# First attention of a two-layer network: projections spaced by three slots, masks and row normalisation moved to GpSimd

## The reference, cut to what matters

```
x = x + _L0_attn_ref(_layernorm(x), w_qkv, b_qkv, w_out, b_out)

def _L0_attn_ref(x, w_qkv, b_qkv, w_out, b_out):          # 16 heads of 16
    q, k, v = jnp.split(x @ w_qkv + b_qkv, 3, axis=-1)
    dot = jnp.einsum('bhid,bhjd->bhij', q, k)
    vals = q_norm_sq + k_norm_sq.transpose(0, 1, 3, 2)
    scores = dot * dot / (vals - 2.0 * dot + EPSILON)
    scores = scores + mask                                # -1e9 above the diagonal
    attn = jax.nn.softmax(scores, axis=-1)
    out = jnp.einsum('bhij,bhjd->bhid', attn, v)
    return out @ w_out + b_out
```

## Time and profile before

| What | Value |
|---|---|
| median of 3 runs | 2801.84 us (2799.59 to 2802.47) |
| the profiled execution, whole | 2797.78 us |
| its span in the trace | 2796.0 us |
| mean granted TensorE clock | 0.976 of full speed |
| busy shares over the span: PE, DVE, ACT, POOL | 94%, 82%, 74%, 65% |
| first `weigh` and last `weigh` of the first attention | 44.12 us and 1295.09 us |

### The profile page before, as it was taken

One profiled execution on the slowest core, in us unless ns is written; L12 is line 12 of the kernel. 1 busy time (PEld: TensorE's weight loads), 2 busy tenths in 40 slices (PEclk: granted clock), 3 DMA queues, 4 the chain that ended last, 5 costly groups with the idle time before them and its releaser, 6 DMA issues. The chain is left out here.

```text
span 2796.0 us, 75274 instructions
## 1 busy us (share of the span) xinstructions
PE 2615.3 (94%) x27044; PEld 1818.8 (65%) x27044; DVE 2280.6 (82%) x6931; ACT 2078.2 (74%) x3782; POOL 1811.9 (65%) x3152
## 2 busy tenths in 40 slices
PE   5999999999999999997889789999999999699999
PEld 3677777777777777775333257777777777466766
DVE  5999999999999999986655468888888888488998
ACT  4998899999998999895333257667677776478886
POOL 3767666777667766774421157677777767588885
PEclk8999999999999999999899889999999999899999
DMA  4334433444334433441000166655556664000001
GB/s 116 68 62 77 79 61 62 74 80 79 61 64 80 73 61 62 72 72 47 10 0 1 32 106 105 105 96 104 97 101 97 104 99 71 1 16 24 24 24 39
DMA packets 110387, 182.21 MB, mean 65 GB/s; under 512 B 27008, under 2 KB 96384, under 8 KB 97920
## 3 DMA queue, kind: packets, MB, share of 16 engines
q1 hardware_dynamic: 106560, 176.61, 34.7%
q10 hardware_dynamic: 3456, 0.79, 0.2%
HBM read 116.25 MB, written 60.29 MB: 63 GB/s over the span
## 5 line engine op out<-in xcount | busy, mean ns | idle before, releaser
L808 POOL TENSOR_TENSOR ratio_scores<-ratio_scores,ratio_max_cols 128x512 f32<-128x512 f32 (+3 forms) x1024 | 726.1, 726 | 319.3 <-DVE ratio_max_cols L718 316.9
L1328 DVE CUSTOM_DVE_ANT_0 zeroed_unused<-bank,zeroed_drop 128x512 bf16<-128x512 f32 (+3 forms) x1024 | 440.0, 484 | 121.1 <-PE bank L198 120.9
L198 PE MATMUL bank<-ratio_k_stack,ratio_q_stack 102*128 102x512 bf16 (+7 forms) x2048 | 506.3, 303 | 33.4 <-DVE ratio_max_cols L718 17.5
L718 DVE CUSTOM_DVE_ANT_0 ratio_scores<-bank,ratio_scores 128x512 f32<-128x512 f32 (+3 forms) x1024 | 472.4, 489 | 22.2
L1216 ACT ACTIVATE zeroed_prob<-bank 128x512 f32<-128x512 f32 x640 | 370.1, 593 | 161.2 <-PE bank L1103 160.3
L580 ACT ACTIVATE ratio_prob<-bank 128x512 f32<-128x512 f32 x640 | 378.4, 592 | 105.5 <-PE bank L494 102.7
L708 DVE TENSOR_TENSOR ratio_scores<-bank,ratio_inverse 128x512 f32<-128x512 f32 x640 | 435.9, 681 | 16.8 <-PE bank L198 9.6
L491 PE MATMUL bank<-const_f_sb,ratio_scores 128*128 128x128 f32 x2560 | 409.9, 274 | 0.9 <-ACT ratio_prob L580 0.9
L569 ACT ACTIVATE ratio_inverse<-bank 128x512 f32<-128x512 f32 x640 | 381.1, 596 | 12.7 <-PE bank L201 12.6
L573 ACT ACTIVATE ratio_inverse<-ratio_inverse 128x1024 f32<-128x1024 f32 x320 | 338.6, 1058 | 10.1
L1446 POOL TENSOR_SCALAR_AFFINE_SELECT zeroed_prob<-zeroed_prob 128x256 f32<-128x256 f32 (+1 forms) x640 | 227.7, 361 | 178.0 <-ACT zeroed_prob L1216 172.2
(11 more groups left out here) (178 smaller groups left out, 5412.6 us busy)
## 6 DMA issues: line engine op xcount, KB each, us to landing
ratio_q_stack<-ratio_parts_q SPq DMA_DIRECT2D x186, 128.0 KB
ratio_k_stack<-ratio_parts_k SPq DMA_DIRECT2D x186, 128.0 KB
zeroed_q_stack<-zeroed_parts_q SPq DMA_DIRECT2D x186, 128.0 KB, 4.7
zeroed_k_stack<-zeroed_parts_k SPq DMA_DIRECT2D x186, 128.0 KB, 7.7
ratio_parts_q<-ratio_parts SPq DMA_DIRECT2D x96, 128.0 KB
ratio_parts_k<-ratio_parts SPq DMA_DIRECT2D x96, 128.0 KB
zeroed_parts_q<-zeroed_parts SPq DMA_DIRECT2D x96, 128.0 KB
zeroed_parts_k<-zeroed_parts SPq DMA_DIRECT2D x96, 128.0 KB
```

The costliest lines, as they stand in the source:

```text
L198: i = e.matmul(bank[:, off:off + w], qs[0:rows, s, hh, ib * P:(ib + 1) * P], ks[0:rows, s, hh, 0:w], start=(k == 0), stop=mask is None, sk ...
L718: i = e.tensor_tensor_reduce(seg, dot_banks[n % 2][:, at], seg, 1.0, 0.0, ALU.mult, ALU.max, mx[:, pair % M_BUFS, c:c + 1])
L808: i = e.tensor_tensor(seg, seg, mx[:, pair % M_BUFS, c:c + 1].to_broadcast([P, w]), ALU.subtract)
L1328: i = e.tensor_tensor_reduce(unused[:, n % 2, at], bank[:, at], drop[:, L - (ib + 1) * P:L], 1.0, 0.0, ALU.add, ALU.max, mx[:, pair % FOLD ...
```

## The change

Five edits, all in the first attention.

1. `PREP_AT`: q stays in slot 2 of a half, k goes from slot 4 to 5, n from 6 to 8; the two values steps (9 and 12, or 9 and 13) become one step "v" of four tiles in slot 12, with one DVE instruction in place of four. DVE does the values, and adds a projected row, one slot later than PE fills the bank. The statistics go from slots 16 and 20 to 17 and 21 (`RATIO_OUT_STATS`).
2. ACT computes the squares one slot after the high part (`square`), once DVE has read the bank for the rest. DVE's rest waits for the high part alone. The bank's next use waits for the squares too (`wait_left`).
3. The mask of a two-block unit is written into the scores by POOL, with one `affine_select` of 128x256 (`mask(n - 1)`, behind `less(n)`), and PE leaves out the mask products of those units. Single units are as before.
4. The normalised row is written by POOL, four instructions of 128x256 in slots 7, 9, 11 and 13 of half 0, into a buffer of four tiles, where DVE wrote it in slots 14 and 18 into one of two.
5. Scores have 9 buffers where they had 10, and an unused mask constant is gone.

```diff
-S_BUFS, INV_BUFS, PROB_BUFS = 10, 6, 13
+S_BUFS, INV_BUFS, PROB_BUFS = 9, 6, 13
-PREP_AT = ({2: "q", 4: "k", 6: "n", 9: "va", 12: "vb", 16: "x0"}, {0: "x1", 2: "q", 4: "k", 6: "n", 9: "va", 13: "vb"})
-R_ROOT_AT, R_XN_AT, R_STATS_AT = 3, (14, 18), (15, 17)
+PREP_AT = ({2: "q", 5: "k", 8: "n", 12: "v", 16: "x0"}, {0: "x1", 2: "q", 5: "k", 8: "n", 12: "v"})
+R_ROOT_AT, R_XN_AT, R_STATS_AT = 3, (7, 9, 11, 13), (15, 17)
-RATIO_BIAS, RATIO_OUT_STATS = (44, 46, 48, 50), (56, 60)
+RATIO_BIAS, RATIO_OUT_STATS = (44, 46, 48, 50), (57, 61)
...
+            elif last[0] == "prep":
+                q.wait_ge(s["prep_read"], last[1])
+                q.wait_ge(s["squares"], ratio_squares(last[1]))
...
-                q.wait_ge(s["lessened"], n + 1)
                 q.wait_ge(s["prob"], n - 1)
...
+                if len(UNITS[n % N_UNITS]) == 1:
+                    q.wait_ge(s["lessened"], n + 1)
...
+                else:
+                    q.wait_ge(s["masked"], masked_by(n))
+                    for t in range(T):
+                        at = slice(t * P, (t + 1) * P)
+                        i = e.transpose(bank[:, at], scores[:, n % S_BUFS, at], net.ident)
+                    i.then_inc(s["turned"])
...
+            def square(half, side):
+
+                b, m = divmod(half, 2)
+                use = ratio_prep(b, f"{sides[side]}{m}")
+                q.wait_ge(s["prep_read"], use)
...
-                step = ratio_prep_at(n, halves)
+                step, late = ratio_prep_at(n, halves), ratio_prep_at(n - 1, halves)
+                if late and late[2] in sides:
+                    square(2 * late[0] + late[1], sides.index(late[2]))
...
             def split(half, side):
                 m, at = half % 2, 2 * half + side
-                q.wait_ge(s["squares"], at + 1)
+                q.wait_ge(s["hi"], at + 1)
...
+                if late and late[2] == "v":
+                    prepare(*late)
+                if step and step[2] != "v":
                     prepare(*step)
...
-                b, step = ratio_row_at(n, B)
+                b, step = ratio_row_at(n - 1, B)
                 if b is not None and step % 2:
                     add_row(b, step // 2)
...
+            def normal(b, t):
+                q.wait_ge(net.x_loaded[b], 16)
+                q.wait_ge(s["rstd"], b + 1)
...
+                e.tensor_scalar(xn[:, t, :], net.x[:, b * T + t, :], net.mean_var[:, b * T + t, 0:1],
+                                net.rstd[:, b * T + t:b * T + t + 1], ALU.subtract, ALU.mult).then_inc(s["xn"])
...
+                q.wait_ge(s["lessened"], n + 1)
+                e.affine_select(diagonal, diagonal, [[0, 2]][:len(blocks) - 1] + [[-1, P]], ALU.is_ge, dropped, 0, 1).then_inc(s["masked"])
```

150 lines of the change are left out of this document (77 added, 73 removed).

## The result

The changed kernel takes **2889.19 us** in the median of 4 runs (2886.80 to 2896.11), against 2800.72 for the kernel before in the same job. The ratio is 1.0321, with a 95% interval of 1.0301 to 1.0341. The forecast was 2809 us and the range ended at 2835: the direction was right, the size was wrong by a factor of more than ten (8 us forecast, 88 measured). One run in all, of the first kernel of experiment 8, took 11952.22 us and is slow; its ratio leaves that run out.

The account below looks back on a forecast made before the run. No engine alone bounds the first attention: whoever is late at each step holds a row of 78.92 us. +0.75 us over 15.5 rows, +11.6, less 1.1 (start) and 2.5 (first row) gives about 2809 us from 2801.84; range 2765 to 2835.

Parts of the forecast that it names:

- The q split: Slot 2 of each half: DVE's rest waits for the high part alone, not the squares; gain 1.1 us a row.
- The k split: k in slot 5, opened only after maxima(3): DVE waits 1.25 us at k in each half; loss 1.75 us a row.
- The norms: After k's high part ACT's queue delays the norms; DVE waits 0.9 us in each half, loss 1.55 us a row.
- The values: Four DVE instructions become one: gain 0.55 us a row; nothing charged for DVE at PE's burst in slot 12.
- Slots 10 to 21: Normalisation and one statistics set leave DVE; 20.5 us from weigh(11) to weigh(21) instead of 21.1, gain 0.6 us a row.
- Slots 22 to 41: Mask products leave PE, mostly where it waits for DVE; ACT's exponentials come earlier; gain 0.3 us a row.
- POOL: Added selects and normalisations bring POOL to 88% of the row and cost nothing.
- gathers: The norms' gather comes later: charged nothing; as a rival, late gathers hold PE and give 2829 us, chance 0.17.
- the waits don't come back: Rival: no new waits replace the old, DVE's removed work counts; 2763 us, from 2735 to 2790, chance 0.30.
- The lock: Rival: DVE's four q and k casts a row slow beside GpSimd, 0.75 us a row; 2821 us, chance 0.08.
- The sum: All terms for a row of the first attention: +0.75 us, with bounds of -0.4 and +1.4 us.
- The bounds 2795 to 2823: Whole-kernel times from the row's bounds of -0.4 and +1.4 us, around the forecast of about 2809 us.

Follow-up runs that it names:

- experiment 8: Kernel before, DVE's and GpSimd's part one slot later: q and k, masks on GpSimd (first kernel), 2795.61 us; norms too, 2798.78; masks on PE, 2802.11 and 2805.50.
- Experiment 2: Changed kernel with the first attend of a group one slot later, slot 6 of a half instead of 5: 2850.49 us, ratio 1.0177.
- experiment 3: Changed kernel with eight products without use added on PE behind the denominators of slot 9: 2857.42 us, ratio 1.0201.
- 4: Changed kernel with the values in two steps again, four DVE instructions, read in the slot in which PE makes them: 2848.99 us, ratio 1.0179.
- experiment 6: Changed kernel with k and n in slots 4 and 6, then rows, values and squares, normalisation taken back in turn; rows 0.54 us a row; masks left, 2796.8 us.
- the kernel with early squares: Changed kernel with edit 2 alone undone, ACT computing the squares right behind the high part: 2893.73 us, ratio 1.0338.
- k alone back: Changed kernel with only the k projection back in slot 4, the norms staying in slot 8: 2844.24 us, ratio 1.0158.
- experiment 1: Changed kernel with k and n back in slots 4 and 6: 2817.05 us, ratio 1.0056; with k back only: 2844.24 us, ratio 1.0158.
- q, k, norms later: Kernel before with DVE's and GpSimd's part of q, k and norms one slot later: 2798.78 us with masks on GpSimd; also run with masks on PE.
- two numbers alone: Kernel before with k in slot 5 and n in slot 8 and nothing else: 2898.43 us, ratio 1.0358.
- experiment 5: Kernel before with only k in slot 5, n in 8: 2898.43 us, with added PE products 2864.81; changed kernel with squares early again: 2893.73 us.

## Why the prediction was wrong, point by point

**The q split** was to gain 1.1 us a row with 0.9 us of wait left. It gained more: slots 2 and 22 went from 8.05 to 6.36 us, with waits of 0.74 and 0.55 us.

**The k split** was to lose 1.75 us, with a wait of 1.25 us. The wait is 1.00 us in both halves; slots 4, 5, 24 and 25 together went from 8.83 to 9.99 us, a loss of 1.16. The chain from `maxima(3)` was the right one, a quarter of a microsecond too long; 0.07 us of that is a sum: its terms add up to 3.93 us, not 4.0.

**The norms** are the step that failed. The prediction gave ACT a full queue from k's high part to the norms' and came to 0.9 us of wait; slots 6 to 8 and 26 to 28 were to lose 1.55 us a row, and they lost 3.6. Its working starts the queue as if ACT could go on at once. But slot 5 is one in which PE has an attend, which slot 4 had not: `turn(0)` comes behind it, and ACT stands 1.15 us first. 0.9 + 1.15 is 2.05; the trace shows 1.99 and 2.03. The queue itself was right: from the end of that wait to the end of the norms' high part ACT takes 6.3 us (forecast 6.25). I counted each instruction that the moved step issues, but not the one that already stood in the slot into which it was moved. Experiment 2 takes that attend away and the wait falls by half a microsecond, not by 1.15, since two attends, of slots 6 and 7, then stand ahead of `turn(2)`, for which ACT waits 0.50 us in slot 8; 0.9 + 0.5 is near the 1.49 that DVE waits:

```profile
627.84 0.60 ACT L596 ACTIVATE ratio_prob<-bank 128x512 f32<-128x512 f32 x1 [0.50 <-PE bank L506]
```

**The clock** was in no step. The prediction read PE as full and didn't ask what it does while DVE waits 2 us in slot 8. Together with the merged values, which took away PE's work in slot 9, that is an idle time of 2.11 us, and the clock costs 32 us (experiment 3): more than the 26 us that the range had above the forecast.

**The values**: "I charge nothing for DVE there" was wrong even at full clock. `dots(13)` waits for the burst, and slot 13 has 2.02 us in every kernel with it and 1.41 without; with what it saves elsewhere the merge comes out nearly even by row (experiment 3 against 4: 82.6 and 82.5 us a row; the whole differs by 8 us, part of it in the first and last rows), and in the changed kernel it loses 2.3 us, nearly all by way of the clock.

**Slots 10 to 21** were to take 20.5 us up to `weigh(21)`. The kernel with values as before and all else changed has just that, 20.55 us. But the set of statistics that was moved out of this stretch had been credited and never charged again. It stands in slot 21, behind PE's crowded stretch, where it is hidden by nothing: 2.98 us in place of 2.01. The rows taken back (experiment 6) gave 0.54 us. At full clock (experiment 3) the values, this stretch and slots 22 to 41, from which 1.45 us were to be gained, lose 0.5 us.

**Slots 22 to 41, POOL and gathers**: the mask products off PE brought nothing to slots 35 to 41 (12.15 us both times), and 0.2 us in the whole row, not 0.3. GpSimd was priced well: the select takes 415 ns and the normalisation 1216 ns, PE's transposes wait 0.4 us for the masks in the whole span, and POOL is busy for 67.8 us a row (159.97 us of 200) where 69.2 were forecast. The gathers never held PE in the changed kernel. The length of its rows is not the reason: the kernel with early squares, at 85.1 us a row, waits 0.65 us a row for them. Why is open.

**The rivals.** That the waits don't come back was refuted by the first look at the waits. The gathers did not decide here; the most that they took in any kernel was the 0.2 us a row of experiment 8, out of 1.27 us that PE waited. The lock hardly acted in the changed kernel either: the rests' casts had a median of 426 ns and the norms' 420, at most 484 and 501, each behind a wait for ACT. But a wait in front is no safeguard: with k alone back (experiment 1) the norms' cast stands behind one of 1.55 us and takes 1.00 us. And the sentence that the rows show 0.19 us and not the length of a POOL instruction holds only for the kernel before. In experiment 8 the cast is longer by 0.84 us and ends 0.3 us behind the instruction of 1.04 us that it met. The Trainium skill, SBUF — State Buffer, section Who interferes with whom, has it that whoever issues first keeps the shared pair of ports for the whole instruction and the other one is blocked; this trace nearly agrees, for the cast ends 0.27 us behind the subtraction, where a whole cast would take 0.42.

**The sum.** The norms were short by 2.1 us a row and the clock, at 2.2 us, was not in it; the gains that did not come at full clock make 2.0 us more, and q and k came out 1.2 us better: 5.0 us between the 0.75 forecast and the 5.76 measured. The bounds 2795 to 2823 leave out the 3.6 us that the forecast takes off for the start and the first row; with them they are 2792 to 2820, which changes nothing in the answer.

## What to carry to other kernels

When a step is moved to another slot, list first what already stands in that slot on each engine, and count from there; a queue that is full does not start before the first thing that it needs. What an edit takes out of one stretch has to be charged where it goes, at the first slot behind it too. And before a wait is removed or a burst merged, ask what it covers: here the half burst in slot 9 covered an idle time of TensorE that costs the clock, and the waits for ACT stood where DVE would else have waited for the next dots, or its cast for GpSimd.

## What the runs showed of the hardware

**Idle times of TensorE of about 2 us are enough to lose the clock.** Counted over PE's timelines from 100 to 1240 us, by the profile's records of the granted clock (worked out; a fall is put down to the idle time next to its start):

```
idle time     kernel                      falls of times
1.4 to 1.5    after, and five more          0 of 162
1.3 to 1.9    q, k, norms later, slot 38    1 of 9 (after 1.86)
1.75          attend one slot later         1 of 14
1.91          two numbers alone            16 of 26
2.03          squares early                14 of 28
2.04          after, slot 30                7 of 14
2.11          after, slot 10               10 of 13
2.11          k alone back                  5 of 14
```

So the idle time alone does not decide it (the same 1.91 us brought 12 falls of 13 in half 0 and 4 of 13 in half 1; why is open), but below 1.6 us there was no fall, and from 1.9 us it came in about half of the cases. The granted clock stayed at 0.50 for 3.4 us each time. A fall cost the row 1.6 to 1.7 us in each of the four places of the table in experiment 5, that is about all of the 1.7 us by which 3.4 us at half the clock put PE behind (worked out): nothing of it was hidden, at the values or at a projection. The Trainium skill, TensorE: Matmul & The Clock Gate, section HAM oscillation, warns of long gaps of waiting for a DMA; the gaps seen here are shorter, and end on VectorE, so for this kernel the measurement decides. That a few microseconds of useless products win 32 us is the same thing seen from the other side.

**A cast of VectorE can take three times its own duration** (1.26 us for 0.42), with no wait shown in front of it, while a GpSimd instruction is under way. It also feeds the clock: in the kernel with k alone back it makes PE's idle time of 1.53 us one of 2.11, and that has falls (experiment 1). Such a wait is found only in the duration of single instructions, minimum against median, and in the timeline of GpSimd beside it.
